# Routed MLP with residual and layer norm: the last group stored by plain DMAs, the one before it by a scatter

## What is computed

```python
out_nr  = gelu(x @ w1_nr + b1_nr) @ w2_nr + b2_nr                        # condition 0
out_tsr = gelu(x @ w1_tsr + b1_tsr) @ w2_tsr + b2_tsr                    # condition 1
out_sr  = gelu(gelu(x @ w1_sr + b1_sr) @ w2_sr + b2_sr) @ w3_sr + b3_sr  # condition 2
y = x + out
result = (y - mean(y)) * rsqrt(var(y) + 1e-5) * gamma + beta             # over the 256 features
```

## Time and profile before

| | |
|---|---|
| time, median of 3 runs | 110.48 us (110.17 to 110.58) |
| time of the profiled execution | 110.82 us |
| its span, first to last instruction | 109.0 us |
| outside the span | 1.82 us |
| PE, DVE, ACT, POOL busy | 81%, 70%, 60%, 61% of the span |
| scatters of POOL (L401) | 8, 1.05 us of POOL each |
| plain stores of 64 KB | 4 on ACTq, 4 on SPq |
| last matrix product starts | 94.58 us |

### The profile page before, as it was taken

One profiled execution on the slowest core, in us unless ns is written; L12 is line 12 of the kernel. 1 busy time (PEld: TensorE's weight loads), 2 busy tenths in 40 slices (PEclk: granted clock), 3 DMA queues, 4 the chain that ended last, 5 costly groups with the idle time before them and its releaser, 6 DMA issues.

```text
span 109.0 us, 1787 instructions
## 1 busy us (share of the span) xinstructions
PE 88.5 (81%) x523; PEld 77.6 (71%) x523; DVE 76.0 (70%) x194; ACT 65.7 (60%) x106; POOL 66.4 (61%) x79
## 2 busy tenths in 40 slices
PE   0269989999999999999999999999999999800000
PEld 0157768868889888898998989989889899700000
DVE  5579085662656672739989999899898979897400
ACT  0994239995986046895967949779597672150000
POOL 6337900029776330006769997879878798989600
PEclk9999999999999999999999999999999999996555
DMA  0895788000498990000004030040220401005282
GB/s 5 277 300 186 228 257 281 15 0 3 132 323 253 398 409 33 0 6 0 0 6 192 9 140 32 9 192 0 110 89 6 192 3 42 21 0 197 47 242 80
DMA packets 5572, 12.85 MB, mean 118 GB/s; under 512 B 800, under 2 KB 2864, under 8 KB 5552
## 3 DMA queue, kind: packets, MB, share of 16 engines
q0 software_dynamic: 2736, 9.44, 23.5%
q1 hardware_dynamic: 2668, 2.89, 8.2%
q10 hardware_dynamic: 148, 0.27, 1.6%
HBM read 8.40 MB, written 4.72 MB: 120 GB/s over the span
## 4 chain that ended last, share of the span: by engine, by line
PE 62%; POOL 14%; ACT 6%; DVE 4%; DMA 4%; issue 3%; ACTq 1%; POOLq 0%; DVEq 0%
PE ps_a L761 7%; PE ps_a L763 7%; PE ps_a L762 7%; PE ps_x L746 6%; PE ps_f L823 6%; PE ps_f L821 6%; PE ps_f L822 6%; POOL xs L393 4%; PE ps_f L862 4%; DMA bias_rows<-L_cond_b_sr_dram 4%; PE ps_f L804 3%; POOL xs L388 3%; POOL out_dram L401 3%; POOL rstd L378 3%; ACT h_hi L457 2%
## 5 line engine op out<-in xcount | busy, mean ns | idle before, releaser
L388 POOL TENSOR_TENSOR xs<-xs,gamma_b 128x768 f32<-128x768 f32 (+1 forms) x8 | 14.3, 1791 | 8.0 <-ACT xs L461 7.8
L823 PE MATMUL ps_f<-wf_hi,f_hi 128*128 x64 | 18.0, 282 | 0.0
L822 PE MATMUL ps_f<-wf_lo,f_hi 128*128 x64 | 18.0, 282 | 0.0
L821 PE MATMUL ps_f<-wf_hi,f_lo 128*128 x64 | 18.0, 282 | 0.0
L457 ACT ACTIVATE f_hi<-ps_a,bias_cols 128x512 fp32r<-128x512 f32 x16 | 11.0, 689 | 9.9 <-PE ps_a L856 4.7
L761 PE MATMUL ps_a<-x_hi,w_lo 128*128 128x512 f32 x40 | 16.6, 415 | 0.3 <-DVE x_lo L685 0.3
L763 PE MATMUL ps_a<-x_hi,w_hi 128*128 128x512 f32 x40 | 15.7, 392 | 0.0
L762 PE MATMUL ps_a<-x_lo,w_hi 128*128 128x512 f32 x40 | 15.6, 391 | 0.0
L349 POOL DMA_INDIRECT xs<-x_dram,load_idx x11 | 11.3, 1029 | 6.4 <-DVE load_idx L578 3.5
L461 ACT ACTIVATE xs<-xs,shift,rstd 128x256 f32<-128x256 f32 x23 | 12.1, 595 | 4.2 <-POOL shift L382 4.2
L458 ACT ACTIVATE ps_a<-ps_a,bias_cols 128x512 f32<-128x512 f32 x22 | 14.4, 654 | 0.0
(11 more groups left out here) (138 smaller groups left out, 190.0 us busy)
## 6 DMA issues: line engine op xcount, KB each, us to landing
w_raw<-L_cond_w_sr_dram SPq DMA_DIRECT2D x2, 512.0 KB, 4.4
wf_raw<-L_cond_w_sr_dram SPq DMA_DIRECT2D x1, 256.0 KB, 5.1
w_raw<-L_cond_w_tsr_dram SPq DMA_DIRECT2D x1, 256.0 KB, 6.7
w_raw<-L_cond_w_nr_dram SPq DMA_DIRECT2D x1, 256.0 KB, 6.9
wf_raw<-L_cond_w_tsr_dram SPq DMA_DIRECT2D x1, 256.0 KB, 7.1
wf_raw<-L_cond_w_nr_dram SPq DMA_DIRECT2D x1, 256.0 KB, 7.2
out_dram<-xs ACTq DMA_DIRECT2D x4, 64.0 KB, 2.4
out_dram<-xs SPq DMA_DIRECT2D x4, 64.0 KB, 3.1
```

Of the source, the lines that this page charges most:

```text
L388: nc.gpsimd.tensor_tensor(tiles, tiles, spread(gamma_b, n), ALU.mult).then_inc(gam_pool, 1)
L821: nc.tensor.matmul(dst, fl[:, kt, toks], w_hi, start=False, stop=False)
L822: nc.tensor.matmul(dst, fh[:, kt, toks], w_lo, start=False, stop=False)
L823: mm = nc.tensor.matmul(dst, fh[:, kt, toks], w_hi, start=False, stop=last)
```

## The change

POOL's last step takes the power of group 8 first, then does gamma and beta of group 7 and scatters group 7, not group 8. SP and ACT store group 8 by plain DMAs, not group 7; they no longer wait for `o_pool`. `scatter` always waits for its `o_pool` and `o_dve`. SP has no waits in its steps; behind its stores it waits for `stored` of groups 0 to 7 and for `stored_next`. At ACT's start GELU on one element comes before the Copy into `ident_r`.

```diff
@@ store_half
             seqs = load_places(eng, seq_regs, 0, g, first, B - 1)
-            eng.wait_ge(o_pool, g + 1)
             eng.wait_ge(o_dve, 2 * (g + 1))
@@ block.sync
-            def sp_step(s):
-
-                if s >= 2:
-                    sp.wait_ge(stored[s - 2], 16)
-
             def sp_finish(g):
-                store_half(sp, seq_regs, taken_regs, g - 1, 0)
+                store_half(sp, seq_regs, taken_regs, g, 0)
+
+                for s in range(g + 1):
+                    if s != g:
+                        sp.wait_ge(stored[s], 16)
                 sp.wait_ge(stored_next, 16 * PER)
-                sp.wait_ge(stored[g], 16)
-
-            each_step(sp, cls, sp_step, sp_finish)
+
+            each_step(sp, cls, lambda s: None, sp_finish)
@@ block.gpsimd
-            def scatter(g, last):
+            def scatter(g):
                 if g == 0:
                     pool.wait_ge(store_idx_done, 1)
-                if not last:
-                    pool.wait_ge(o_pool, g + 1)
+                pool.wait_ge(o_pool, g + 1)
                 pool.wait_ge(o_dve, 2 * (g + 1))
@@ pool_group
-                    scatter(g - 1, False)
+                    scatter(g - 1)
             def pool_finish(g):
+
+                root(g)
                 times_gamma(g - 1, 2)
-                root(g)
                 plus_beta(g - 1, 2)
-                scatter(g, True)
+                scatter(g - 1)
@@ block.scalar
+            nc.scalar.activation(warm[:, :], ident[0:1, 0:1], ACT.Gelu)
             nc.scalar.activation(ident_r[:, :], ident[:, :], ACT.Copy).then_inc(ident_done, 1)
-            nc.scalar.activation(warm[:, :], ident[0:1, 0:1], ACT.Gelu)
@@ act_finish
-                store_half(act, seq_regs, taken_regs, g - 1, PER // 2)
+                store_half(act, seq_regs, taken_regs, g, PER // 2)
```

## The result

The changed kernel takes 110.12 us (median of 10 runs, 109.86 to 110.79), the kernel before, run beside it, 110.75 (10 runs, 110.17 to 111.72). The ratio is 0.9943, 95% interval 0.9916 to 0.9969: faster by 0.6%, where 1.2% had been forecast. The profiled execution took 109.96 us, 108.2 of it the span.

The account below looks back on a forecast made before the run. PE bounds the first 95 us, SP's late stores of group 7 the end. Last landing 106.5 instead of 107.9, plus 1.1, gives span 107.7, a gain of 1.3; time 109.2, range 108.0 to 110.5.

Parts of the forecast that it names:

- Power first: POOL's power of group 8 ahead of gamma: DVE's 0.71 us wait goes, the last group is complete 0.69 us earlier.
- Issue times: Tail: plain stores of group 8 first issue at 101.59 on both queues, SP's fourth at 103.5, POOL's scatter at 101.96.
- Landing times: Tail: SP's fourth store lands at 106.5; the scatter of group 7, given 4.6 us, at 106.56.
- Volume check: Tail: 0.983 MB at 275 GB/s takes 3.57 us from 102.4; plus about 0.5 to a landing gives 106.5.
- What bounds the kernel before: End of the kernel: SP's stores of group 7, begun 1.65 us behind a late landing, end it at 107.9.
- Scatter of group 6 held up by a fetch: Its landing took 4.7 us, 1.3 above the median; a 16 KB fetch on the instruction queue was held for the cause.
- ACT's start: GELU before Copy removes one table load of 1.28 us; worth nothing, since ACT idles 3.34 us for PE's transposes.
- SP's waits at the end: Nine semaphore waits behind SP's stores: at most 0.3 us, covered by the landings at 106.5.
- DRAIN: POOL's DRAIN at the end of the block ends 5.42 us behind the scatter's start, at 107.38.
- Rival 2: The scatter of group 7 meets stores and a fetch, landing at 107.9 as before; time 110.5, chance 0.17.

Follow-up runs that it names:

- SP freed alone: The kernel before with one edit: SP doesn't wait in its steps, only behind its stores; ratio 0.9965, tail 12.83 us.
- all plain: The changed kernel with groups 6 and 7 also stored by plain DMAs, so no scatter in the tail; 111.77 us, ratio 1.0103.
- group 6 plain too: The changed kernel with group 6 also stored by plain DMAs, four on SP and four on ACT; 109.20 us, ratio 0.9822.

## Why the prediction was off

The measured median, 110.12, is 0.9 above the forecast 109.2. The steps in turn:

- *Power first.* Right to a few hundredths. The wait of 0.71 is gone; L670 starts at 99.09, 2.98 behind L664, where 3.08 had been worked out (99.60 - 96.52).
- *Issue times.* Right: SP's first store at 4.96 (forecast 5.07), its fourth at 6.95 (6.98), the scatter at 5.42 (5.44).
- *Landing times.* This step failed. The scatter was given 4.6, the time of the one scatter at the end of before; it took 5.4, in all three profiles (5.4, 5.4, 5.5), against 3.4 with no store beside it. Its packets begin 1.9 us behind the issue (1.6 alone) and then run for 2.9 us (1.4 alone). Last landing 10.83 behind L664 against 9.98 forecast: 0.85 us, all but 0.1 of the miss. In the third profile a plain store landed 0.17 behind the scatter, at 11.02. I took a duration measured in one arrangement of three queues into another, in which all seven plain stores are issued before the first packet of the scatter; before, three of SP's four came later. The spread of 3.1 to 4.7 had the warning.
- *Volume check.* It failed with it, and should not have been called a third route: 275 GB/s was the rate of the plateau, and I let it run from the first packet. At the start of the burst it is mostly plain stores that move, at 172 to 176 GB/s after; before, the first stretch has 61. The trace had that row, and I used it only for a starting time.
- *What bounds the kernel before.* SP's 1.65 us of late start were in the chain of the profile, but not the price of it. Freed alone, SP's stores went out 2 us earlier and the last landed at 11.59, against 11.31, 12.27 and 12.34 before. What an engine waits for last and what it costs are two things: the earlier issue was real and the landing didn't follow. The Trainium skill ("DMA: Bandwidth & Descriptors", section "Issuing engines are not separate DMA queues") says that DMAs of all issuing engines run on the same 16 DMA engines and interleave, so that issuing from several saves issue time only. The trace of SP freed alone agrees: 2 us of earlier issue, and a last landing 0.3 behind that of the first profile of before and 0.7 ahead of the other two. I cited it and still counted the earlier issue in full.
- *Scatter of group 6 held up by a fetch.* Borne out by the traces, but not isolated. It took 3.6 to 5.0 us in the 17 profiles in which group 6 is scattered, and each has a packet of 16 KB on the instruction queue beside it. The later that fetch ends, the later the scatter lands: 1.3 and 1.35 us behind the scatter's start for the two that landed after 3.6, 2.9 for the one that took 5.0 (correlation 0.89 over the 17). No run here takes the fetch away. SP's waits on it don't decide the end in any case.
- *ACT's start, SP's waits at the end, DRAIN.* Right for the first (no gain) and the last (in this kernel the DRAIN ended at 107.76, ahead of SP's at 108.0). SP's waits were put at nothing; from the last landing to the end it took 1.30 where it was 1.17 before, the 0.1 that is left of the miss.
- *Rivals.* None was what happened. Rival 2 came nearest: the collision is its mechanism, without the fetch that it wanted. The collision was in the kernel before as well, and worse in most of its executions than in the one I set out from (12.49 against 12.7 from the medians), which would explain why a gain of 0.6 us remained and not the 0.36 of the two first profiles.

**What stays open.** What sets the rate of the mixture. Bytes don't do it alone: a scatter alone runs at 422 GB/s, the mixture at 299 with the engines 79 to 95% busy. Nor is it a fixed fee, since three stores less gave 0.57 us and a scatter 0.82 us later cost nothing. Engine time adds up to part of it: 0.524 MB at 422 / 1.03 = 410 GB/s is 1.3 us, 0.459 MB at 205 / 0.85 = 241 GB/s is 1.9 us; that sum, 3.2, began near 102.0 and would have ended at 105.2, while packets ran until 106.4. Why the bytes of one plain queue cost twice those of the other is a part of the same question. The Trainium skill's rule that an engine drains a whole packet of one ring before it turns to another (same page, "Queues, rings and completion order") would hold plain stores behind a scatter; no run here isolates it. Why two tails of before were 13.5 and two 12.5 to 12.7 is open as well.

## What to carry to other kernels

Where several queues write at once at the end of a kernel, price each kind alone and all together on the chip before crediting an earlier issue: a duration from issue to landing belongs to the arrangement in which it was measured. The larger gain here (1.8% against 0.6%) came with taking a transfer out of POOL's chain and giving it to idle queues, so that the scatter of group 7 goes ahead of group 8's stores, and not from issuing the same burst sooner; how much each half of that brought isn't shown. And profile a tail of some microseconds more than once before forecasting from it: two further profiles of the kernel before had tails a microsecond longer.

## What the runs showed of the hardware

- A plain store of 64 KB out of 16 partitions lands 1.9 us behind its issue (the last one, with the last scatter left out and with all plain), up to 2.3 where two queues issue together; the last landing was 4.2 behind the last issue beside a scatter of 7 sequences, 0.46 MB (SP freed alone). Stores of one semaphore can be matched to their landings only in the order of issue.
- With the last scatter left out, each 4 KB packet of ACT's stores kept a DMA engine for 0.16 us, and those of SP's stores, issued at the same time, for 0.16 to 0.6 (mean 0.36). A packet of the scatter alone took 0.16.
- A scatter of 128 rows of 4 KB lands 3.4 us behind its start alone, 3.7 to 5.6 with 7 or 8 plain stores in the tail, and moves 422 GB/s where plain stores from two queues move 205, each in its busiest stretch.
- POOL's DRAIN at the end of the block ended 0.82 us behind the landing of its last scatter in four profiles (landings at 105.64, 106.87, 106.91 and 106.94), and took 2.2 us with nothing of POOL's in flight (all plain).
- From the last landing to the end of the span it took 0.9 us (group 6 plain too) to 1.3 us (after), and 1.47 with all plain stores.
